# Cross-attention and a quantised gated FFN in one kernel: who multiplies the down product's scale, VectorE or GpSimd

## What is computed

```python
def _quant_weight(w):
    scale = jnp.mean(jnp.abs(w)) + EPS
    wq = jnp.clip(jnp.round(w / scale), -1.0, 1.0)
def _quant_act(x):
    s = jnp.max(jnp.abs(x), axis=-1, keepdims=True) / 127.0 + EPS
    xq = jnp.clip(jnp.round(x / s), -128.0, 127.0)
def _qlinear(x, w):
    y = jnp.einsum('bsi,oi->bso', xq, wq)
    return y * xs * ws
gate = jax.nn.silu(_qlinear(x, w_gate))
up = _qlinear(x, w_up)
return _qlinear(gate * up, w_down)
```

## Time and profile before

| What | Value |
|---|---|
| Median of 3 runs | 91.2 us (90.95 to 91.27) |
| The profiled execution's own time | 91.3 us |
| Its span, first to last instruction | 89.5 us |
| Granted TensorE clock | full (1.000) throughout |
| Busy: TensorE, VectorE, ScalarE, GpSimd | 78.3, 71.5, 59.2, 55.3 us (88, 80, 66, 62% of the span) |

### The profile page before, as it was taken

One profiled execution on the slowest core, in us unless ns is written; L12 is line 12 of the kernel. 1 busy time (PEld: TensorE's weight loads), 2 busy tenths in 40 slices (PEclk: granted clock), 3 DMA queues, 4 the chain that ended last, 5 costly groups with the idle time before them and its releaser, 6 DMA issues.

```text
span 89.5 us, 2414 instructions
## 1 busy us (share of the span) xinstructions
PE 78.3 (88%) x872; PEld 56.8 (63%) x872; DVE 71.5 (80%) x181; ACT 59.2 (66%) x99; POOL 55.3 (62%) x108
## 2 busy tenths in 40 slices
PE   4987877999999999999999999989778996998580
PEld 1476654779797887879777786556133672765360
DVE  4738688298698987979689899399999998999550
ACT  2461159979772799675897789907448696886600
POOL 5632479899997935979475600250799636759640
PEclk9999999999999999999999999999999999999999
DMA  1979999800000000007307300900000000101224
GB/s 32 259 226 306 303 374 371 319 33 4 0 7 0 0 7 0 0 0 174 71 0 168 74 0 0 234 7 0 0 0 0 0 0 4 51 15 51 66 73 161
DMA packets 11511, 7.59 MB, mean 85 GB/s; under 512 B 6540, under 2 KB 11244, under 8 KB 11500
## 3 DMA queue, kind: packets, MB, share of 16 engines
q1 hardware_dynamic: 11084, 7.05, 26.4%
q10 hardware_dynamic: 416, 0.39, 1.3%
HBM read 4.95 MB, written 0.92 MB: 66 GB/s over the span
## 4 chain that ended last, share of the span: by engine, by line
PE 55%; DVE 30%; issue 6%; ACT 5%; POOL 1%; DVEq 0%
PE bank L945 23%; PE sc L945 15%; DVE amax L860 9%; DVE h_sb L853 8%; PE bank L1090 8%; PE bank L1114 3%; ACT probs L584 2%; ACT kT L569 2%; PE bank L1025 2%; PE bank L998 2%; PE bank L1017 1%; DVE k_wide L675 1%; DVE ctxT L672 1%; DVE s_tok L867 1%; DVE probs L764 1%
## 5 line engine op out<-in xcount | busy, mean ns | idle before, releaser
L945 PE MATMUL sc<-wT,xqT 128*128 128x512 bf16 x56 | 14.0, 380 | 1.3 <-DVE h_sb L853 1.3
L300 POOL TENSOR_TENSOR k_wide<-kT,head_mask 128x896 f32<-128x896 f32 (+1 forms) x8 | 11.7, 1493 | 0.0
L515 POOL TENSOR_SCALAR y_int<-y_sb,r_tok 128x256 f32<-128x256 f32 x7 | 3.4, 479 | 13.3 <-DVE r_tok L828 7.5
L853 DVE SCALAR_TENSOR_TENSOR h_sb<-sc,s_out,wf_sb 128x512 f32<-128x512 f32 x14 | 10.0, 740 | 1.6 <-ACT wf_sb L630 1.6
L630 ACT ACTIVATE wf_sb<-sc,s_out 128x512 f32<-128x512 f32 x14 | 9.3, 686 | 2.5 <-PE sc L945 1.9
L313 POOL TENSOR_SCALAR wf_sb<-h_sb,r_tok 128x512 f32<-128x512 f32 x13 | 9.1, 714 | 2.4 <-DVE r_tok L874 2.4
L755 DVE TENSOR_REDUCE mx<-sc 128x16 f32<-128x896 f32 x8 | 8.7, 1088 | 1.5 <-PE sc L945 1.5
L584 ACT ACTIVATE probs<-probs 128x896 f32<-128x896 f32 x8 | 7.6, 952 | 3.3 <-DVE probs L764 3.3
L945 PEld LDWEIGHTS sc<-wT,xqT 128*128 128x128 bf16 x56 | 5.0, 98 | 7.2 <-DVE h_sb L853 3.5
L945 PEld LDWEIGHTS bank<-v_wide,pT 128*64 128x64 f32 x256 | 8.1, 138 | 2.1 <-issue 2.0
L945 PE MATMUL bank<-v_wide,pT 128*64 128x34 f32 x256 | 9.0, 225 | 0.1
(11 more groups left out here) (109 smaller groups left out, 169.5 us busy)
## 6 DMA issues: line engine op xcount, KB each, us to landing
wf_sb<-in_L_ffn_w_gate_dram SPq DMA_DIRECT2D x1, 1024.0 KB, 8.6
wf_sb<-in_L_ffn_w_up_dram SPq DMA_DIRECT2D x1, 1024.0 KB, 10.8
wf_sb<-in_L_ffn_w_down_dram SPq DMA_DIRECT2D x1, 1024.0 KB, 12.7
out_dram<-k_wide SPq DMA_DIRECT2D x7, 128.0 KB, 1.7
x_sb<-in_x_dram SPq DMA_DIRECT2D x1, 384.0 KB, 6.2
x_sb<-in_x_dram SPq DMA_DIRECT2D x2, 128.0 KB, 3.0
wq_sb<-in_L_xattn_Wq_dram ACTq DMA_DIRECT2D x1, 256.0 KB, 3.0
x_sb<-in_x_dram SPq DMA_DIRECT2D x1, 256.0 KB, 3.7
```

What stands on the lines that cost most here:

```text
L300: ops.tensor_tensor(k_wide[:, c, hf, :, cols], kT[:, c, hf, None, cols].to_broadcast([P, RH, n]), head_mask[:, 0:RH, None].to_broadcast([P ...
L853: nc.vector.scalar_tensor_tensor(h_sb[:, t % 3, cols], SC[:, j % 4, :], s_out[:, 1, t:t + 1], g_sb[:, t % 2, cols], ALU.mult, ALU.mult).th ...
L945: return nc.tensor.matmul(*a, **k)
```

## The change

The multiplication that makes the down product's scale leaves VectorE's invert_gated_scales and becomes a function of GpSimd, called in every slot behind the two roundings and ahead of the residual. It waits for the token scale and for the weight scale's bank read, and raises the same semaphore.

```diff
@@ gpsimd
+            def down_scale(s):
+                t = s - GU0
+                if 0 <= t < NT:
+                    pool.wait_ge(h_scale_ready, t + 1)
+                    wait_read(pool, ("mean", 2))
+                    nc.gpsimd.tensor_tensor(s_out[:, 2, t:t + 1], s_tok[:, 1, t:t + 1], w_scale[:, 2:3],
+                                            ALU.mult).then_inc(dn_scale_ready, 1)
...
                 second_layer_norm(s)
                 round_gated(s, 0)
                 round_gated(s, 1)
+                down_scale(s)
                 add_residual(s)
...
@@ vector, invert_gated_scales
                     dve.wait_ge(h_scale_ready, t + 1)
                     nc.vector.reciprocal(r_tok[:, 1, t:t + 1], s_tok[:, 1, t:t + 1]).then_inc(r_ready, 1)
-                    wait_read(dve, ("mean", 2))
-                    nc.vector.tensor_tensor(s_out[:, 2, t:t + 1], s_tok[:, 1, t:t + 1], w_scale[:, 2:3],
-                                            ALU.mult).then_inc(dn_scale_ready, 1)
```

## The result

The changed kernel takes 90.42 us (median of 7 runs, 90.13 to 90.81) against 91.2 us before, a ratio of 0.990 with a 95% interval of 0.988 to 0.993. It is faster by 0.8 us, twice what I forecast, and on the other side of the bound of 0.5%: the likeliest case was "same", and the result is rival C's, down to its number (a gain of 0.77 us, 90.4).

The account below looks back on a forecast made before the run. VectorE was taken to set the pace from 60.33 us to the last reciprocal at 83.31. Five steps of 0.06 plus 0.15 for tile 2 gave 0.45 us off 91.2, forecast 90.8 us, range 90.4 to 91.4.

Parts of the forecast that it names:

- rival C: On VectorE: the multiply's whole duration goes (1.07 us, 90.1) or the 0.32 us hole closes (0.77 us, 90.4); chance 0.17.
- VectorE's unexplained hole of 0.32 us before line 835 at 74.21 I leave as it is: VectorE's idle 0.32 us ahead of line 835 at 74.21 was left unchanged and given no share of the gain.
- The size of the removal: VectorE without line 876: 0.06 us in each of tiles 0, 1, 3, 4, 5, 0.15 in tile 2, sum 0.45 us.
- the step behind the reciprocal stays about the same: On VectorE, line 876's successor would start 0.07 to 0.08 us behind the reciprocal, so line 876's own step goes away.
- The bound from whole durations (1.07): On VectorE: if each line 876's whole duration were on the path, the gain would be 6 x 0.14 + 0.23 = 1.07 us.
- the 227 ns row: Tile 2's line 876 on VectorE, 227 ns against 140, ending with GpSimd's pair of roundings; its removal was counted at 0.15 us.
- Tile 6 at nothing: Tile 6's line 876 lies inside the wait of VectorE's rounding for the reciprocal, so removing it gains nothing.
- GpSimd at nothing: The seven 128x1 multiplies added to GpSimd would cost no time, covered by idle time and later waits.
- The price taken, 0.27: Time of one added GpSimd multiply, taken as 0.27 us, with 0.15 kept as lower and 0.76 as upper bound.
- The covers named: GpSimd idle time taking up the multiplies: 0.89 us before 70.47, 0.49 us in tile 4, 0.96 us in tiles 5 and 6.
- Rival B: Tile 1's GpSimd multiply or rounding contends with VectorE's two-input line 835 near 69.87, giving back up to 0.41 us; 91.1; chance 0.18.
- Rival D: Each GpSimd multiply stops VectorE's line 853 or 860 beside it in six tiles: +1.2 us, 92.4; chance 0.10 with the hole.

Follow-up runs that it names:

- the runs with more moved: The changed kernel with the gate and up scales of tiles 4 to 6 also on GpSimd: 90.31 us with 10 waits ahead of slot 8, 91.01 us without.
- the first experiment: The kernel before with 16 long-met waits added to VectorE's list ahead of slot 8, in idle time: 91.01 us, ratio 0.997.
- the run with line 835 as number 256: The kernel before with 128 long-met waits (64 wait instructions) ahead of slot 8 on VectorE: 96.77 us, one execution.

## Why the prediction was wrong

**The step that failed** is "VectorE's unexplained hole of 0.32 us before line 835 at 74.21 I leave as it is". It belongs to instruction 192 of VectorE's list, and the change takes four instructions out ahead of it, so it fell on the wait ahead of the second product of a pair of 1.39 us, where it does not show. The sum put it at nothing; it is 0.33 of the 0.72 us. Rival C named it, at part of a chance of 0.17, "an accident of position". Counting the list before and after would have shown ahead that anything tied to number 192 falls beside a long instruction, and that C was worth more than that; that the hole is tied to the number took the runs. Without the hole's share the gain would have been 0.39 us, inside the forecast's 0.3 to 0.5.

**The size of the removal** was 0.45 in the sum and measures 0.38 to 0.40. Tiles 0 to 3 gave what the distances between starts said (0.07, 0.05, 0.16 and, less the hole, 0.06). The step that failed here is "the step behind the reciprocal stays about the same": in tiles 4 and 5 it is 0.11 and 0.10 instead of 0.08, so each gave 0.03 or less. Why is not shown. From tile 3 on the gated product waits for a third semaphore, which fits the 0.10 to 0.11 of all later tiles in the runs with more moved; but in the changed kernel, where the multiply of line 844 still stands ahead of the reciprocal, tiles 3 and 4 keep 0.08 and 0.07 in spite of it. The bound from whole durations (1.07) was far off, and the 227 ns row was on the path with 0.15, as taken: moving that multiply alone shortened the stretch by 0.17.

**Tile 6 at nothing** held: the tail is 3.55 and 3.56 us.

**GpSimd at nothing** held with room: once, twice and not at all give stretches of 22.34, 22.34 and 22.33 us. The price taken, 0.27, was too high; 0.19 for the instruction and 0.14 for its follower were measured, just below the lower bound of 0.15. The covers named took it up, ahead of the roundings of tiles 4 to 6 and in the idle time behind tile 1 (0.37 of 0.89 left).

**Rival B** did not occur, but narrowly: the multiply of tile 1 ran from 69.60 to 69.79, and the two-input line started at 69.83 and took 0.16. The run with two multiplies put the pair across each other without a trace of it, as far as that run can tell. The Trainium skill's "SBUF — State Buffer", section "Who interferes with whom", would have the two contend; the one-column pair at 69.93 does not show it, the long rows agree with it. The 227 ns row ends with GpSimd's roundings (69.59 and 69.58). It came back in the first experiment, where both end at 71.71; in the run with 256 waits a row of line 876 takes 0.36 us and ends at 145.17, with GpSimd's normalisation at 145.16; and with GpSimd idle beside it tile 2's multiply takes 0.14. So 0.09 of the 0.15 us that tile 2 gave was contention, and the prediction was right to price it apart. **Rival D** is out: lines 862 and 869 take 732 to 752 and 1208 to 1220 ns, as before.

## What to carry to other kernels

Price a short instruction on a bound engine by the distance between starts, not by its duration: here 0.06 against 0.14 us, and even that came back only in part in two of the tiles, where the step behind the reciprocal grew. Before you credit or blame an edit for a few tenths of a microsecond, look for holes that no semaphore explains, and count where they stand in the engine's list; an edit that adds or takes instructions ahead moves them, and a few waits in idle time move them back, which is a cheap control. A small operation whose inputs are ready before those of the work it stands beside is free on an engine that waits anyway, ahead of that work or behind it.

## What was not expected of the hardware

VectorE stalls at instruction 192 of its list when it gets there through a chain of short instructions (four kernels: 0.25 to 0.37 us beyond the usual step), at 320 too (0.27), and not visibly at 256; at 192 under a long instruction it does not show (six kernels). In each of the five an instruction packet of 8 KB follows within a microsecond. In the kernel before, the DMA view of 74.8 to 75.1 us has

```profile
q14 instruction: 1, 0.01, 9.9%
```

as its only packet, 0.7 us behind the hole, and none between 73.9 and 74.25, in the hole itself. The packet comes with the place and not with the hole: the six kernels in which number 192 is hidden have it too (at 74.73 in the changed kernel, a microsecond into its long pair), and in the run with line 835 as number 256 no such packet follows that line; the last of 8 KB is at 61.8 us, among the waits, where number 192 lies. The Trainium skill's "Runtime: NRT & Kernel Launch", section "Instruction fetch mechanics", says that the sequencer fetches its list in blocks of 16 KiB, 256 instructions, by its own DMA queue and that crossing a block is mostly hidden. The packet agrees with a fetch of this kind. The spacing of 128 does not agree with that block size, though by the Trainium skill's figures 8 KB would hold 128 instructions (an estimate), and a third of a microsecond on a bound engine is not hidden. That the crossing causes the hole is argued from this; what the engine does in it was not shown.
